# The input stage of a Mamba layer: one fp32 projection against three products of scaled fp16 parts

## The chip, the core and the metric

The kernel runs on one core of one Trainium2 chip. The core has five engines, each with its own queue of instructions: TensorE (PE: matmuls, and PEld: its weight loads), VectorE (DVE), ScalarE (ACT), GpSimd (POOL) and SyncE (SP, which here issues nearly all DMAs). They wait for one another through semaphores only. The metric is the device time of one launch in microseconds; lower is better.

## What is computed

A macaron block over x of shape (4, 2048, 256): half an attention and mixture-of-experts layer, a Mamba layer, and half an attention and mixture-of-experts layer again. The change touches only the first part of the Mamba layer, for which the reference says:

```python
h = _layernorm(_layernorm(x), norm_w, norm_b)
xz = jnp.einsum('bld,ed->bel', h, in_proj_w)        # 256 channels in, 1024 out
x, z = jnp.split(xz, 2, axis=1)                     # 512 each; x is convolved and scanned, silu(z) gates
# out = x_in + the layer's output, x_in being the first layer norm of the block's stream
```

With the norm's weight and bias written out, xz = W (w * a + b) = (W w) a + W b, where a is the normed row without weight and bias.

## The kernel before

The program is a row of phases with a barrier between them: constants, the first attention layer (three phases), `mamba_in`, two scans (forward and backward), `mamba_out`, and the second attention layer (three phases). `mamba_in` (from L1222) works on 8192 rows in 16 chunks of 512 rows. For chunk i:

- SP loads the rows (0.5 MB) into `xs`, stores `bs` (0.5 MB, stream plus normed rows, read again by `mamba_out`), `xo` (1 MB) and `zo` (1 MB). All have two buffers, by the chunk's parity.
- DVE: `statistics` (L1308) computes mean and variance and the two inverse variances; `norm` (L1327) makes the normed rows `sn` and the twice normed rows `an`; `add_base` (L1338) makes `bs`; `weigh` (L1342) reads the turned rows from PSUM, applies the norm's weight and bias, and writes `aT`; `copy_x` (L1350) moves one 128x512 tile of the x half from PSUM to `xo`, four times.
- PE: `turn` (L1380) transposes the 512x256 rows in eight 128x128 blocks; `project` (L1392) makes one 128x512 tile of the output from two fp32 matmuls (contraction 256 = 2 x 128), eight times for a chunk: x and z by turns for m = 0 to 3.
- ACT: `root` (L1412) takes the square roots of the inverse variances; `silu` (L1417) moves one tile of the z half from PSUM to `zo`, four times.
- POOL has no work in this phase.

The order is written out by hand and is the same for every chunk. PE's step i: wait for `aT` of chunk i; x0, z0, x1, z1, then `turn(i + 1)`, then x2, z2, x3, z3. DVE's step i: copy x0, norm(i + 1), copy x1, add_base(i + 1), weigh(i + 1), copy x2, statistics(i + 2), copy x3. ACT's step i: four silus, then root(i + 2). The x tiles go by turns to PSUM banks 2 and 3, the z tiles to banks 4 and 5, so a tile's matmuls wait until the tile two before it has been read. Before the first step each engine runs a prologue with the same pieces for chunk 0 and statistics(1).

The later attention phase `ffn_out` already computes its experts with three products of fp16 parts: there ACT copies the turned rows from PSUM twice (L1091 to fp32, L1094 to fp16), POOL subtracts (L983), and PE multiplies (L1045) 128x512 tiles, with other stationary operands for every matmul. `make_constants` (L81) prepares the expert weights in the same manner.

## Time and profile before

| what | value |
|---|---|
| median of 3 runs | 8745.64 us (8745.47 to 8752.05) |
| profiled execution, its own time | 8750.53 us |
| its span | 8748.8 us |
| PE, DVE, ACT, POOL busy over the span | 84%, 86%, 58%, 42% |
| the phase `mamba_in` | from about 2386 to about 2642 us of the span |

Spans of the trace are counted from the span's start. A busy PE is one whose pipeline holds a matmul; the time between the starts of two matmuls says what one of them costs. An fp32 matmul stands in the trace as two records, a transpose as one. Busy shares over the whole span mix eleven phases, so what the change is worth has to be read inside its own phase.

### The profile page before, as it was taken

What the parts mean: (1) busy time and instruction counts of PE and PEld (TensorE: products, weight loads), DVE (VectorE), ACT (ScalarE), POOL (GpSimd) and SP (SyncE); (2) the same over time, 40 slices, a digit from 0 to 9 for tenths busy, and PEclk for the clock granted to TensorE, in tenths of its full rate; (3) what the DMA queues carried; (4) which work ended last, traced back from release to release, by engine and by line L of the source; (5) the groups of instructions that cost most, each with busy time, mean ns of one, the idle gap of its engine ahead of it and who ended that gap; (6) DMA issues with size and microseconds to landing.
All of it is one profiled execution on the core that took longest, in us unless ns stands there. A gap on an engine that the chain in (4) does not pass through costs nothing. (4 is left out here: it accounts for less than half of the span.)

```text
span 8748.8 us, 137191 instructions
## 1 busy us (share of the span) xinstructions
PE 7384.9 (84%) x39098; PEld 2876.4 (33%) x39098; DVE 7557.3 (86%) x11017; ACT 5055.9 (58%) x7663; POOL 3676.0 (42%) x1812
## 2 busy tenths in 40 slices
PE   6788888889997888888878888888777888888799
PEld 3222222225543333333323333333542222222255
DVE  6898888878867999999979999999358988888888
ACT  3577777762235666666655555555224777777622
POOL 0010011100006999999969999999300100110000
PEclk8799999999999999999999999999987999999999
DMA  6001001012262222222223333333561011011122
GB/s 171 17 19 20 19 19 26 19 42 77 72 210 88 83 83 82 82 83 84 83 92 100 102 103 100 100 102 100 171 189 17 19 20 19 19 21 23 42 67 67
DMA packets 554170, 623.35 MB, mean 71 GB/s; under 512 B 205376, under 2 KB 363328, under 8 KB 549408
## 3 DMA queue, kind: packets, MB, share of 16 engines
q1 hardware_dynamic: 548896, 581.63, 22.8%
q0 software_dynamic: 4608, 33.56, 1.9%
q8 instruction: 330, 5.41, 0.3%
q14 instruction: 336, 2.75, 0.1%
HBM read 416.65 MB, written 163.76 MB: 66 GB/s over the span
## 5 line engine op out<-in xcount | busy, mean ns | idle before, releaser
L833 DVE TENSOR_REDUCE ffn_att_mx<-psum 128x1 f32<-128x512 f32 (+2 forms) x4840 | 2915.6, 655 | 389.7 <-PE psum L666 197.4
L794 ACT ACTIVATE ffn_att_e<-psum,unscale 128x1024 f32<-128x1024 f32 (+3 forms) x2560 | 2384.0, 983 | 843.9 <-PE psum L739 842.9
L632 POOL TENSOR_SCALAR_AFFINE_SELECT ffn_att_e<-ffn_att_e 128x512 f32<-128x512 f32 x512 | 324.6, 634 | 3125.8 <-ACT ffn_att_e L794 3125.8
L666 PE MATMUL psum<-ffn_att_k,ffn_att_q 48*128 48x512 f16 (+3 forms) x5384 | 989.1, 368 | 611.2 <-DVE ffn_att_mx L833 545.2
L1628 POOL TENSOR_TENSOR scan_r_h<-scan_r_h,scan_r_cs 128x1024 f32<-128x1024 f32 x512 | 1207.1, 2447 | 148.0 <-ACT scan_r_state L1791 144.7
L705 PE MATMUL psum<-ffn_att_e,ffn_att_v 128*32 128x512 f32 (+3 forms) x10240 | 1248.5, 558 | 10.0 <-issue 3.8
L1628 POOL TENSOR_TENSOR scan_f_h<-scan_f_h,scan_f_cs 128x1024 f32<-128x1024 f32 x512 | 1204.4, 2444 | 118.8 <-ACT scan_f_state L1791 116.1
L1707 PE MATMUL psum<-scan_f_h,ident 128*128 128x512 f32 x2048 | 989.0, 623 | 84.0 <-POOL scan_f_h L1628 83.1
L1707 PE MATMUL psum<-scan_r_h,ident 128*128 128x512 f32 x2048 | 975.0, 617 | 78.1 <-POOL scan_r_h L1628 77.5
L1831 ACT ACTIVATE psum<-scan_r_dt,scan_r_an 128x512 f32<-128x512 f32 x1024 | 698.1, 682 | 456.2 <-DVE scan_r_h L1923 456.0
L1831 ACT ACTIVATE psum<-scan_f_dt,scan_f_an 128x512 f32<-128x512 f32 x1024 | 697.6, 681 | 423.8 <-DVE scan_f_h L1923 423.3
L666 PEld LDWEIGHTS psum<-ffn_att_k,ffn_att_q 48*128 48x128 f16 x5384 | 263.9, 94 | 2002.3 <-DVE ffn_att_mx L833 1884.7
L1923 DVE TENSOR_TENSOR_SCAN scan_r_h<-psum,scan_r_state,scan_r_db 128x512 f32<-128x512 f32 x704 | 844.5, 1261 | 5.5 <-ACT psum L1831 5.5
L1923 DVE TENSOR_TENSOR_SCAN scan_f_h<-psum,scan_f_state,scan_f_db 128x512 f32<-128x512 f32 x704 | 840.5, 1261 | 9.0 <-ACT psum L1831 9.0
L739 PE MATMUL psum<-ffn_att_q,ffn_att_k 50*128 50x512 f16 (+3 forms) x5120 | 728.1, 355 | 32.9 <-issue 29.5
L1707 PEld LDWEIGHTS psum<-scan_f_h,ident 128*128 128x128 f32 x2048 | 384.7, 197 | 670.2 <-issue 434.1
L1707 PEld LDWEIGHTS psum<-scan_r_h,ident 128*128 128x128 f32 x2048 | 383.9, 195 | 648.8 <-issue 439.2
L1180 DVE SCALAR_TENSOR_TENSOR ffn_out_acc<-psum,ffn_out_comb,ffn_out_acc 128x256 f32<-128x256 f32 x896 | 433.4, 484 | 65.2 <-PE psum L1045 29.6
L1889 DVE TENSOR_TENSOR scan_r_db<-scan_r_du,psum 128x2048 f32<-128x2048 f32 x177 | 404.9, 2288 | 25.1 <-PE psum L1682 4.8
L1889 DVE TENSOR_TENSOR scan_f_db<-scan_f_du,psum 128x2048 f32<-128x2048 f32 x177 | 404.9, 2288 | 24.7 <-DVE scan_f_h L1923 3.9
L1923 DVE TENSOR_TENSOR_SCAN scan_f_h<-psum,scan_f_state,scan_f_dbp 128x512 f32<-128x512 f32 x320 | 385.9, 1264 | 30.8 <-ACT psum L1831 30.8
L1923 DVE TENSOR_TENSOR_SCAN scan_r_h<-psum,scan_r_state,scan_r_dbp 128x512 f32<-128x512 f32 x320 | 385.9, 1264 | 30.8 <-ACT psum L1831 30.8
(240 smaller groups left out, 9216.5 us busy)
## 6 DMA issues: line engine op xcount, KB each, us to landing
scan_f_cs<-scan_f_bcd SPq DMA_DIRECT2D x264, 256.0 KB, 3.2
scan_r_cs<-scan_r_bcd SPq DMA_DIRECT2D x264, 256.0 KB, 3.3
scan_f_bs<-scan_f_bcd SPq DMA_DIRECT2D x82, 256.0 KB, 3.5
scan_r_bs<-scan_r_bcd SPq DMA_DIRECT2D x82, 256.0 KB, 3.5
scan_f_win<-xp SPq DMA_DIRECT2D x18, 1036.0 KB, 6.6
scan_r_win<-xp SPq DMA_DIRECT2D x18, 1036.0 KB, 7.0
ffn_att_q<-q_parts SPq DMA_DIRECT2D x144, 128.0 KB, 2.9
mamba_out_ys<-yz SPq DMA_DIRECT2D x18, 1024.0 KB, 7.3
```

The lines of the kernel that those rows point to most:

```text
L632: nc.gpsimd.affine_select(out=part, in_=part, compare_op=ALU.is_ge, fill=0.0, base=0, pattern=[[0, REP], [1, P]], channel_multiplier=-1).t ...
L666: ins = nc.tensor.matmul(psum[:, turns[hh], j * w:(j + 1) * w], q[at, i // HALF, pair, i % HALF * P:(i % HALF + 1) * P], k[at, c * P:c * P ...
L705: ins = nc.tensor.matmul(psum[32 * h:32 * h + VW, BANK_O, off:CH], V[par][:, kb, :], E[:, s % PB, h, off:CH], start=kb == 0, stop=closes(s ...
L739: ins = nc.tensor.matmul(psum[:, h, off:CH], k[at, kb * P:(kb + 1) * P], q[at, qb * CH // (HALF * P), h // 2, qb * CH % (HALF * P) + off:q ...
L794: nc.scalar.activation(E[:, s % PB, 2 * hp:2 * hp + 2, off:CH], psum[:, 2 * hp:2 * hp + 2, off:CH], ACT.Exp, scale=unscale[:, 0:1]).then_i ...
L833: nc.vector.reduce_max(mx[:, hh * 2 + pairs[0]:hh * 2 + pairs[1], i // HALF, i % HALF, c // TT], psum[:, turn, 0:(pairs[1] - pairs[0]) * w ...
L1180: nc.vector.scalar_tensor_tensor(acc[:, e % 2, :], psum[:, BANKS_E[(n // 2) % 4], (e % 2) * C:(e % 2 + 1) * C], comb[par][:, t, e:e + 1], ...
L1628: nc.gpsimd.tensor_tensor(hh, hh, cs[:, n % NCS, :].unsqueeze(1).to_broadcast([P, 2, CH]), ALU.mult).then_inc(hc_ready, 1)
L1707: ins = nc.tensor.matmul(psum[:, m, :], ident[:, :], h[n % NH][:, m, :], start=False, stop=n == DS - 1)
L1831: nc.scalar.activation(psum[:, BANK_A + k % 2, :], dt[par][:, m, :], ACT.Exp, scale=an[:, m, n:n + 1]).then_inc(decay, 1)
L1889: nc.vector.tensor_tensor(db[b_turn(par, n)][:, :, :], du[par][:, :, :], psum[:, BANK_B, :].unsqueeze(1).to_broadcast([P, DM, CH]), ALU.mu ...
L1923: nc.vector.tensor_tensor_scan(h[n % NH][:, m, flip], psum[:, BANK_A + k % 2, flip], made_b[:, m, flip], state[:, n, m:m + 1], ALU.mult, A ...
```

## The change

The two operands of the projection are each written as a sum of two fp16 numbers, high and low, after scaling. The weights: W w, scaled by a factor from the largest row norm, gives `wh` and `wl`, made once, in the prologue. The rows: ACT copies the turned rows times 512 from PSUM as fp32 (`aT`) and as fp16 (`ah`), and POOL subtracts the two to give `al`. `project` makes wh·ah + wl·ah + wh·al, six fp16 matmuls for a tile where there were two fp32 matmuls. The norm's weight is now in the weights and its bias in `beta` = W b, so `weigh` is gone, and `copy_x` and `silu` apply the scale `uw` and the bias `beta` on the way out. `aT` has one buffer now, `ah` and `al` two. The factor needs sums of squares (ACT, then PE), a maximum (DVE), a root (ACT), and `beta` needs 16 small matmuls; all of that stands in the prologue.

```diff
-        aT = [sb(f"aT{p}", [P, CK, CH]) for p in range(2)]
+        aT = sb("aT", [P, CK, CH])
+        ah = [sb(f"ah{p}", [P, CK, CH], F16) for p in range(2)]
+        al = [sb(f"al{p}", [P, CK, CH], F16) for p in range(2)]
+        wh, wl = sb("wh", [P, CK, 2 * DI], F16), sb("wl", [P, CK, 2 * DI], F16)
+        sqb, onesb = sb("sqb", [P, CK, 2 * DI], BF16), sb("onesb", [P, P], BF16)
...
-                def weigh(i, par):
-                    dve.wait_ge(aT_ps, i + 1)
-                    if not (isinstance(i, int) and i < 2):
-                        dve.wait_ge(z_ps, DM * (i - 1))
+                def weights():
+                    dve.wait_ge(w_sums, 2)
+                    nc.vector.reduce_max(most[:, :], psum[:, 6:8, :].rearrange("p b n -> p (b n)"), AX.X).then_inc(w_most, 1)
+                    dve.wait_ge(w_root, 1)
+                    nc.vector.tensor_scalar(root_w[:, :], root_w[:, :], 1.0 / FULL, 1e-15, ALU.mult, ALU.add).then_inc(w_small, 1)
+                    dve.wait_ge(w_small, 2)
+                    nc.vector.reciprocal(cw[:, :], root_w[:, :]).then_inc(w_small, 1)
+                    nc.vector.tensor_scalar(uw[:, :], root_w[:, :], 1.0 / UP, None, ALU.mult).then_inc(w_small, 1)
+                    dve.wait_ge(w_small, 4)
+                    nc.vector.tensor_tensor(sc[:, :], wn[:, :], cw[:, :].to_broadcast([P, CK]), ALU.mult).then_inc(w_small, 1)
+                    dve.wait_ge(w_small, 5)
                     for k in range(CK):
-                        nc.vector.tensor_scalar(aT[par][:, k, :], psum[:, k, :], wn[:, k:k + 1], bn[:, k:k + 1],
-                                                ALU.mult, ALU.add).then_inc(aT_sb, 1)
+                        dve.wait_ge(w_high, k + 1)
+                        nc.vector.scalar_tensor_tensor(wl[:, k, :], wi[:, k, :], sc[:, k:k + 1], wh[:, k, :], ALU.mult, ALU.subtract
+                                                       ).then_inc(w_low, 1)
+                    dve.wait_ge(beta_ps, 1)
+                    nc.vector.tensor_copy(beta[:, :], psum[:, 2, 0:2 * DM]).then_inc(beta_sb, 1)
...
-                    nc.vector.tensor_copy(xo[par][:, m, :], psum[:, X_BANKS[m % 2], :]).then_inc(x_ready, 1)
+                    nc.vector.tensor_scalar(xo[par][:, m, :], psum[:, X_BANKS[m % 2], :], uw[:, 0:1], beta[:, m:m + 1],
+                                            ALU.mult, ALU.add).then_inc(x_ready, 1)
                 statistics(0, 0)
                 norm(0, 0)
                 add_base(0, 0)
-                dve.wait_ge(w_in, 48)
-                weigh(0, 0)
+                weights()
                 statistics(1, 1)
+                dve.wait_ge(beta_sb, 1)
...
                     if nxt:
                         add_base(i + 1, 1 - par)
-                        weigh(i + 1, 1 - par)
...
+            @block.gpsimd
+            def _(pool):
+                def split_low(i, par):
+                    pool.wait_ge(a_high, i + 1)
+                    if not (isinstance(i, int) and i < 2):
+                        pool.wait_ge(z_ps, DM * (i - 1))
+                    nc.gpsimd.tensor_tensor(al[par][:, :, :], aT[:, :, :], ah[par][:, :, :], ALU.subtract).then_inc(a_low, 1)
+                split_low(0, 0)
...
             @block.tensor
             def _(pe):
                 pe.wait_ge(w_in, 48)
+                pe.wait_ge(w_small, 1)
+                pe.wait_ge(w_squares, CK)
+                for b in range(2):
+                    for k in range(CK):
+                        ins = nc.tensor.matmul(psum[:, 6 + b, :], onesb[:, :], sqb[:, k, b * CH:(b + 1) * CH], start=k == 0, stop=k == CK - 1)
+                    ins.then_inc(w_sums, 1)
+                for m in range(2 * DM):
+                    for k in range(CK):
+                        ins = nc.tensor.matmul(psum[:, 2, m:m + 1], wi[:, k, m * P:(m + 1) * P], bn[:, k:k + 1], start=k == 0, stop=k == CK - 1)
+                ins.then_inc(beta_ps, 1)
...
-                        ins = nc.tensor.matmul(psum[:, bank[m % 2], :], wi[:, k, at:at + P], aT[par][:, k, :],
-                                               start=k == 0, stop=k == CK - 1)
+                        for p, (w, a) in enumerate(((wh, ah[par]), (wl, ah[par]), (wh, al[par]))):
+                            ins = nc.tensor.matmul(psum[:, bank[m % 2], :], w[:, k, at:at + P], a[:, k, :],
+                                                   start=k == 0 and p == 0, stop=k == CK - 1 and p == 2)
                     ins.then_inc(made, 1)
 
                 def step(i, par, nxt, more):
-                    pe.wait_ge(aT_sb, CK * (i + 1))
+                    pe.wait_ge(a_high, i + 1)
+                    pe.wait_ge(a_low, i + 1)
...
+                pe.wait_ge(w_low, CK)
+                pe.wait_ge(beta_sb, 1)
                 phase_steps(pe, step)
...
-                    nc.scalar.activation(zo[par][:, m, :], psum[:, Z_BANKS[m % 2], :], ACT.Silu).then_inc(z_ready, 1)
+                    nc.scalar.activation(zo[par][:, m, :], psum[:, Z_BANKS[m % 2], :], ACT.Silu, bias=beta[:, DM + m:DM + m + 1], scale=uw[:, 0:1]
+                                         ).then_inc(z_ready, 1)
+
+                def parts(i, par):
+                    act.wait_ge(aT_ps, i + 1)
+                    act.wait_ge(a_low, i)
+                    nc.scalar.activation(aT[:, :, :], psum[:, 0:CK, :], ACT.Copy, scale=UP).then_inc(aT_sb, 1)
+                    if not (isinstance(i, int) and i < 2):
+                        act.wait_ge(z_ps, DM * (i - 1))
+                    nc.scalar.activation(ah[par][:, :, :], psum[:, 0:CK, :], ACT.Copy, scale=UP).then_inc(a_high, 1)
+                act.wait_ge(w_in, 48)
+                for k in range(CK):
+                    nc.scalar.activation(sqb[:, k, :], wi[:, k, :], ACT.Square, scale=wn[:, k:k + 1]).then_inc(w_squares, 1)
                 root(0)
+                act.wait_ge(w_most, 1)
+                nc.scalar.activation(root_w[:, :], most[:, :], ACT.Sqrt).then_inc(w_root, 1)
+                act.wait_ge(w_small, 5)
+                for k in range(CK):
+                    nc.scalar.activation(wh[:, k, :], wi[:, k, :], ACT.Copy, scale=sc[:, k:k + 1]).then_inc(w_high, 1)
+                parts(0, 0)
                 root(1)
+                act.wait_ge(beta_sb, 1)
 
                 def step(i, par, nxt, more):
                     for m in range(DM):
                         silu(i, par, m)
+                        if nxt and m == 1:
+                            parts(i + 1, 1 - par)
```

Declarations of semaphores are left out; eleven are new. The orders of SP and of the stores are not changed.

## Rows read from the trace of the kernel before

**Rows 1.** Engines by stretch: length, busy us (instructions) of each, PE clock, DMA share, GB/s.

```profile
2386.00:2400.00 14.00, 2.40 (x9) 2.04 (x10) 8.40 (x28) 1.49 (x2) 0.00 (x0) 0.50 0.51 164
2400.00:2636.00 236.00, 234.92 (x632) 110.00 (x631) 155.64 (x423) 78.55 (x108) 0.00 (x0) 0.99 0.60 203
```

**Rows 2.** Waits in the phase: waiting and releasing line, us in total, times, longest.

```profile
PE psum L1397 <- DVE mamba_in_aT L1347: 1.8, 1, 1.8
```

**Rows 3.** PE in order of time, one chunk and a bit: start us, length us.

```profile
2496.41 1.04 PE L1385 MATMUL psum<-ident,mamba_in_an 128*128 128x128 f32 x8
2497.28 13.90 PE L1397 MATMUL psum<-mamba_in_aT,mamba_in_wi 128*128 128x512 f32 x32
...
2511.89 6.60 PE L1397 MATMUL psum<-mamba_in_aT,mamba_in_wi 128*128 128x512 f32 x15
```

**Rows 4.** PE in the earlier phase ffn_out: eleven fp16 matmuls, first and last.

```profile
2369.72 0.38 PE L1045 MATMUL psum<-ffn_out_eh,ffn_out_uh 128*128 128x512 f16 x1
...
2371.88 0.38 PE L1045 MATMUL psum<-ffn_out_el,ffn_out_uh 128*128 128x512 f16 x1
```

**Rows 5.** ACT and POOL splitting turned rows in ffn_out, in order of time.

```profile
2324.12 1.02 ACT L1091 ACTIVATE ffn_out_uT<-psum 128x1024 f32<-128x1024 f32 x1 [3.97 <-PE psum L1022]
2325.04 1.02 ACT L1094 ACTIVATE ffn_out_uh<-psum 128x1024 f16<-128x1024 f32 x1
...
2326.22 2.12 POOL L983 TENSOR_TENSOR ffn_out_ul<-ffn_out_uT,ffn_out_uh 128x1024 f16<-128x1024 f32 x1 [25.50 <-ACT ffn_out_uh L1094]
```

**Rows 6.** DVE in one chunk: norm, and weigh after the turn.

```profile
2487.36 0.18 DVE L1318 RECIPROCAL mamba_in_rq<-mamba_in_va 128x4 f32<-128x4 f32 x1
...
2492.07 1.38 DVE L1330 TENSOR_SCALAR mamba_in_sn<-mamba_in_xs,mamba_in_mv,mamba_in_rs 128x256 f32<-128x256 f32 x4
2493.35 1.14 DVE L1335 TENSOR_SCALAR mamba_in_an<-mamba_in_sn,mamba_in_rs 128x256 f32<-128x256 f32 x4
...
2497.48 1.53 DVE L1347 TENSOR_SCALAR mamba_in_aT<-psum,mamba_in_wn,mamba_in_bn 128x512 f32<-128x512 f32 x2 [0.77 <-PE psum L1385]
```

**Rows 7.** ACT around a root, in order of time.

```profile
2504.35 0.60 ACT L1421 ACTIVATE mamba_in_zo<-psum 128x512 f32<-128x512 f32 x1 [2.84 <-PE psum L1397]
2504.96 1.28 ACT L1415 ACT_TABLE_LOAD   x1
2506.26 0.21 ACT L1415 ACTIVATE mamba_in_rs<-mamba_in_rq 128x8 f32<-128x8 f32 x1
```

**Rows 8.** Groups of the phase: count, busy us, mean ns of one, idle before.

```profile
L1354 DVE COPY mamba_in_xo<-psum 128x512 f32<-128x512 f32 x64 | 44.0, 688 | 61.6 <-PE psum L1397 61.6
L1347 DVE TENSOR_SCALAR mamba_in_aT<-psum,mamba_in_wn,mamba_in_bn 128x512 f32<-128x512 f32 x32 | 24.5, 806 | 11.9 <-PE psum L1385 11.9
```

**Rows 9.** One stretch of 1 us inside a chunk, columns as in rows 1.

```profile
2505.00:2506.00 1.00, 1.00 (x4) 0.51 (x3) 0.00 (x0) 1.00 (x1) 0.00 (x0) 1.00 1.02 383
```

**Rows 10.** The phase's start in order of time, all engines.

```profile
2388.23 0.43 SPq L1274 DMA_DIRECT2D mamba_in_wi<-in_m_inT  x1
...
2393.89 1.38 DVE L1330 TENSOR_SCALAR mamba_in_sn<-mamba_in_xs,mamba_in_mv,mamba_in_rs 128x256 f32<-128x256 f32 x4 [0.28 <-ACT mamba_in_rs L1415]
...
2396.23 1.22 DVE L1340 TENSOR_TENSOR mamba_in_bs<-mamba_in_xs,mamba_in_sn 128x1024 f32<-128x1024 f32 x1
...
2399.54 9.38 PE L1397 MATMUL psum<-mamba_in_aT,mamba_in_wi 128*128 128x512 f32 x16 [1.78 <-DVE mamba_in_aT L1347]
```

**Rows 11.** DMA issues: KB each, median us from issue to landing.

```profile
mamba_in_wi<-in_m_inT SPq DMA_DIRECT2D x1, 1024.0 KB, 7.2
```

**Rows 12.** In the constants phase: squares, a maximum, scaled copies.

```profile
11.45 3.90 ACT L135 ACTIVATE const_sqe<-const_we,const_en 128x2048 bf16<-128x2048 f32 x2 [2.88 <-DMA const_we<-in_f_expT]
...
16.62 1.47 DVE L177 TENSOR_REDUCE const_moste<-psum 128x2 f32<-128x512 f32 x2 [7.06 <-PE psum L154]
...
20.69 6.49 ACT L141 ACTIVATE const_eh<-const_we,const_sc 128x256 f16<-128x256 f32 x16 [0.91 <-DVE const_sc L186]
```

**Rows 13.** PE in ffn_out: eight fp32 matmuls of eight columns.

```profile
2326.51 1.85 PE L1032 MATMUL psum<-ffn_out_wg,ffn_out_uT 128*128 128x8 f32 x16
```

More of the change, by code:

```diff
@@ L1232, in mamba_in @@
         bs = [sb(f"bs{p}", [P, TT, C]) for p in range(2)]
-        aT = [sb(f"aT{p}", [P, CK, CH]) for p in range(2)]
+        aT = sb("aT", [P, CK, CH])
[3 more added lines that the diff above has]
+        sqb, onesb = sb("sqb", [P, CK, 2 * DI], BF16), sb("onesb", [P, P], BF16)
+        most, root_w, cw, uw = (sb(n, [P, 1]) for n in ("most", "root_w", "cw", "uw"))
+        sc, beta = sb("sc", [P, CK]), sb("beta", [P, 2 * DM])
         xo = [sb(f"xo{p}", [P, DM, CH]) for p in range(2)]
@@ L1246, in mamba_in @@
         aT_ps, aT_sb, x_ps, z_ps = sem("aT_ps"), sem("aT_sb"), sem("x_ps"), sem("z_ps")
+        a_high, a_low = sem("a_high"), sem("a_low")
+        w_squares, w_sums, w_most, w_root, w_small, w_high, w_low, beta_ps, beta_sb = (sem(n) for n in (
+            "w_squares", "w_sums", "w_most", "w_root", "w_small", "w_high", "w_low", "beta_ps", "beta_sb"))
         x_ready, z_ready, zeroed = sem("x_ready"), sem("z_ready"), sem("zeroed")
@@ L1306, in _ @@
                 nc.vector.memset(zero[:, :, :], 0.0).then_inc(zeroed, 1)
+                nc.vector.memset(onesb[:, :], 1.0).then_inc(w_small, 1)
                 def statistics(i, par):
@@ L1374, in _, with step @@
                 phase_steps(dve, step)
+            @block.gpsimd
[6 more added lines that the diff above has]
+                split_low(0, 0)
+                def step(i, par, nxt, more):
+                    if nxt:
+                        split_low(i + 1, 1 - par)
+                phase_steps(pool, step)
             @block.tensor
@@ L1378, in _ @@
                 pe.wait_ge(w_in, 48)
+                pe.wait_ge(w_small, 1)
[8 more added lines that the diff above has]
+                ins.then_inc(beta_ps, 1)
                 def turn(i):
-                    pe.wait_ge(aT_sb, CK * i)
+                    pe.wait_ge(a_high, i)
                     for t in range(TT):
```

## Prediction

> **What bounds the kernel now.** The change lies in one phase, so I read that phase and not the shares of the whole span. First the engines by stretch [rows 1]: from 2400 to 2636 us PE is busy 234.92 of 236 us, at a granted clock of 0.99, while DVE is busy 155.64, ACT 78.55 and POOL not at all. A busy PE could still be one that is fed late, so next the waits [rows 2]: in the whole phase PE waits for the turned rows once, 1.8 us, at the start. Then PE in order of time [rows 3]: the projection starts at 2497.28 and again at 2511.89, so a chunk costs 14.61 us; the eight transposes take 0.87 (2496.41 to 2497.28), and the 32 records of the 16 fp32 matmuls the other 13.74. PE sets the pace, DVE has 155.64/236 x 14.61 = 9.6 us of work in a chunk, ACT 4.9.
>
> The start is different. The first projection record begins at 2399.54 [rows 10], with the clock at half (0.50 [rows 1]), and this first half chunk lasts 9.21 us until its transposes instead of half of 13.74, 2.3 more. As a check: 2399.54 + 16 x 14.61 - 0.87 (no turn in the last step) + 2.3 = 2634.7; the phase's PE work ends close to that, just before 2636.
>
> **The change, part by part: the loop.** PE: six fp16 matmuls per tile, 48 a chunk. Eleven such matmuls in ffn_out, each with another stationary operand, start from 2369.72 to 2371.88 [rows 4]: 2.16/10 = 0.216 us each, weight loads hidden. 48 x 0.216 = 10.37, plus 0.87 for the turn (left as it is) = 11.24 us, if nothing else is late. That saves 3.37 us a chunk, 16 x 3.37 = 53.9 us.
>
> What has to fit into 11.24 us? Let the chunk start at 0. A tile takes 1.30, so z1 is done at 5.18, the turn ends at 6.05, and the next chunk wants its `ah` and `al` at 11.24.
>
> The hand-over, the tightest. In the old kernel `weigh` starts 0.20 after the turn's end and needs 1.53 [rows 6]. Now ACT copies twice and POOL subtracts, the same operations in the same shapes as in ffn_out [rows 5]: the second copy starts 0.92 after the first, the subtraction 1.18 after that, and takes 2.12. Sum 0.20 + 0.92 + 1.18 + 2.12 = 4.42. The cover is x2, z2, x3, z3, 24 x 0.216 = 5.18. It fits with 0.76 to spare, so I cost it at nothing; without that cover it would be 4.42 a chunk. Silu z1 is queued in front of the copies on ACT, but it starts at 5.4 and ends at 6.0, before they are released. Behind them stands silu z2, due at 8.8; the copies end at 8.2.
>
> The norm of the next chunk. On ACT silu z3 of the chunk before ends at 0.8; then table load 1.28 and root 0.21 [rows 7] give 2.3. DVE's `norm` takes 2.42 (2492.07 to 2494.49 [rows 6]), so it ends near 4.8, and the turn comes at 5.18; its first block needs only the first quarter of `an`, at about 4.0. It fits, with 0.4 or more to spare.
>
> DVE: minus `weigh`, 1.53; `copy_x` grows from 0.69 to what `weigh` took for one 128x512 tile with two column operands, 0.81 [rows 8], so + 0.5 a chunk. 9.6 - 1.5 + 0.5 = 8.6 of 11.24. ACT: + 1.02 + 1.02, and four silus with scale and bias, which no row shows: 0.60 as now [rows 7] or 0.69, the old copy's; I take 0.65. 4.9 + 2.0 + 0.2 = 7.1 of 11.24. POOL 2.1. The x and z banks: every tile's reader ends at least 1 us before the bank is wanted. All hidden behind PE.
>
> Does a Copy between two silus make ACT load a table? No row has this pair. In ffn_out the copies follow other functions with no load in front of them [rows 5]; nothing is my value. The other end is a load of 1.28 [rows 7] before the copies: the hand-over becomes 5.70, 0.52 late, 8 us over 15 chunks.
>
> DMA: no transfer is added or moved. A chunk still moves 3.15 MB. Now that is 203 GB/s [rows 1]; in 11.24 us it is 280. Inside a chunk the queues reach 383 GB/s at a full share [rows 9] and then stand still, so 3.15/0.383 = 8.2 us of transfer fit. Stores have a whole chunk to land, loads more. Hidden.
>
> **The change: the prologue.** Here nothing hides. Old: weights issued at 2388.23, landing 7.2 later [rows 10, 11], 2395.4; `norm` from 2393.89; projection at 2399.54. New, along the longest chain:
> - ACT waits for the weights, then squares 2 x 1024 columns. 2048 columns took 1.95 [rows 12]; half that and a fixed part, 1.1 each: 2397.6. root(0) is queued behind them, and needs its table after Square: 1.28 + 0.21, 2399.1. So `norm` starts at 2399.15, 5.3 late.
> - From `norm`'s start to the end of `add_base` took 3.56 (2393.89 to 2397.45 [rows 10]): 2402.7.
> - The maximum over 1024 columns stands behind `add_base` on DVE: two of 512 took 1.47 [rows 12], I take 1.3: 2404.0. PE's sums were ready long before.
> - Root 0.25, then four dependent small operations of 0.2 (0.18 and the gap [rows 6]): 2405.1.
> - `wh`: 256 columns took 0.41 [rows 12]; 1024 I take at 1.1, the mean of a plain 1.02 [rows 5] and a bit more; twice: 2407.3.
> - parts(0) and the subtraction, 0.92 + 1.18 + 2.12 = 4.2: 2411.5. With half a microsecond for semaphores the projection starts at 2412.0.
>
> Beside it: `beta`'s 16 matmuls, 32 records. Sixteen of eight columns took 1.85 [rows 13] at full clock, so 3.7, or 7.4 at half; with four matmuls of sums in front and the first turn behind they end between 2404 and 2408.5. `wl` runs on DVE until 2408.7 (1.22 for a tile of this size [rows 10]), `beta`'s copy and statistics(1) after it until 2411.8. None is later than 2412, but PE at half clock comes within a microsecond of the copies.
>
> Cost 2412.0 - 2399.54 = 12.5. Bounds: 10 if the clock has risen for the first chunk too (it would give back 2.3), 16 if PE's own chain at half clock decides and ACT's pieces come out at their upper ends. What the half clock costs in the first chunk I take as the same 2.3, since PE stands still before it in both kernels.
>
> The end of the phase is as before (last stores, then the barrier); eleven more semaphores to clear, 0 to 0.5, taken at 0. Nothing behind the phase reads other data.
>
> **Table loads: row and rule.** The profile shows no time between a silu's end (2504.95), the table load and the root at 2506.26 beyond the load's 1.28 [rows 7]. The Trainium skill (ScalarE: Activation LUTs, What ACT_TABLE_LOAD costs) counts a drain of 1.38 us with each switch; by that the prologue would be an estimated 1.4 us longer. The trace does not agree with it here, so it gets no chance of its own.
>
> **Rivals.** A, the forecast: PE alone sets the pace, 11.24 a chunk.
>
> B, the hand-over or the norm is late. What speaks for it: only 0.76 and some 0.4 us of room, and POOL enters a loop in which DVE reads SBUF. If the subtraction has to stand behind a DVE operation of two SBUF tensors, the longest is `add_base`, 1.22 [rows 10]: 1.22 - 0.76 = 0.46 late, 15 x 0.46 = 7 us. Against: `add_base` should be over at 6.9 and the subtraction start at 8.4. With the table load 8. With both, (1.22 + 1.28 - 0.76) x 15 = 26. So B gives 8711 to 8730, centre 8713. The Trainium skill has a rule for this (SBUF — State Buffer, Who interferes with whom): a GpSimd instruction and a DVE one with two SBUF inputs exclude each other for their whole length. It names a mechanism for B; in the order above they don't meet.
>
> C, DMA becomes the limit. The mean before is 203 GB/s; if it couldn't go over, say, 226, a chunk would take 13.9, the loop would win 11 and the prologue lose 12.5: 8747, no change. Against it stands 383 in the bursts [rows 9].
>
> D, the other side: fp16 products are not at 0.216 here, because every one has its own weight load and would have to end before the next begins. It decides from (14.61 - 0.87 - 12.5/16)/48 = 0.27 us each. With the record's own length, 0.38 [rows 4], as the interval: 48 x 0.38 + 0.87 = 19.1 a chunk, 8745.6 + 16 x 4.5 + 12.5 = 8830. Against: the same rows show such a sequence, with changing weights, at 0.216.
>
> **How the numbers follow.** Saving 53.9 - 12.5 = 41.4. The profiled execution took 8750.5, 4.9 more than the median of the runs; its like would be 8709.1, and on the median 8745.6 - 41.4 = 8704. The likeliest case's own range is 8698 to 8711: the prologue's bounds give - 2.5 and + 3.5, rounding of the matmul interval and the runs' own scatter the rest. Chances: A 0.70; B 0.19, of it 0.16 below 8728; C and anything else that eats the gain 0.06; D or another loss 0.05. The range that leaves out no more than 2 in 10 reaches from 8698 into B, to 8722. A measurement of this kernel tells some 0.2% (17 us) from no change, so faster is below 8728: A and most of B, 0.86; within 0.2%: 0.09; slower: 0.05.
>
> **What would show it.** In the new trace: projection starts 11.2 apart, matmuls 0.216 apart; PE without waits in the loop; the first projection near 2412, its last near 2593; POOL's subtraction ending 4.4 after the turn; no table load between silu and copy. Wrong would make it: PE waiting for POOL or ACT in every chunk; a prologue over 16; a granted clock under 1 in the loop; matmuls further apart.

## The result and the profile after

| | before | after |
|---|---|---|
| median of 4 runs each, beside one another | 8745.56 us (8740.5 to 8752.05) | 8700.63 us (8693.87 to 8704.81) |
| ratio to before | | 0.9945, 95% interval 0.993 to 0.9959 |
| profiled execution, own time and span | 8750.53, 8748.8 us | 8693.87, 8692.0 us |
| `mamba_in`, first load to first load of the scan | 255.7 us | 215.8 us |
| the same chunk, turn to turn | 14.61 us | 11.23 us |
| projection starts after the phase's first load | 12.8 us | 26.2 us |
| second attention, first load of `ffn_in` to load of `ffn_out`'s weights | 1900.8 us | 1882.2 us |

The changed kernel is faster by 45 us in this comparison, and by 65 and 49 us in two later ones. The predicted saving was 41.4 us. The engines by stretch, columns as in [rows 1], over the prologue and the body of the phase in the changed kernel:

```profile
2386.00:2412.00 26.00, 9.91 (x43) 9.00 (x44) 12.61 (x41) 8.01 (x9) 0.62 (x1) 0.50 0.47 123
2412.00:2590.00 178.00, 176.26 (x865) 87.07 (x866) 140.90 (x384) 116.84 (x135) 33.42 (x16) 0.98 0.76 261
```

PE is still what fills the body, 176.26 of 178 us; DVE has 140.90 and ACT 116.84. DMA moves 261 GB/s at a share of 0.76, against 203 before [rows 1], and nothing waits for it there. PE in order of time, the rows that answer to [rows 3]:

```profile
2488.70 1.04 PE L1429 MATMUL psum<-ident,mamba_in_an 128*128 128x128 f32 x8
2489.57 0.38 PE L1442 MATMUL psum<-mamba_in_ah,mamba_in_wh 128*128 128x512 f16 x1
...
2494.76 0.38 PE L1442 MATMUL psum<-mamba_in_ah,mamba_in_wh 128*128 128x512 f16 x1
...
2499.93 1.04 PE L1429 MATMUL psum<-ident,mamba_in_an 128*128 128x128 f32 x8
```

Two turns are 11.23 us apart, two matmuls 0.216 ((2494.76 - 2489.57)/24). The 24 matmuls after the turn end, and the next chunk starts, at 2494.76. The waits of the phase say the same: all that PE waits for in front of its projection is one wait, at the start.

```profile
PE psum L1442 <- POOL mamba_in_al L1402: 4.4, 1, 4.4
```

The other engines in the same chunk, in order of time:

```profile
2488.91 0.78 ACT L1469 ACTIVATE mamba_in_zo<-psum,mamba_in_beta,mamba_in_uw 128x512 f32<-128x512 f32 x1 [0.79 <-PE psum L1442]
2489.85 1.02 ACT L1475 ACTIVATE mamba_in_aT<-psum 128x1024 f32<-128x1024 f32 x1 [0.17 <-PE psum L1429]
2490.77 1.02 ACT L1478 ACTIVATE mamba_in_ah<-psum 128x1024 f16<-128x1024 f32 x1
...
2491.95 2.13 POOL L1402 TENSOR_TENSOR mamba_in_al<-mamba_in_aT,mamba_in_ah 128x1024 f16<-128x1024 f32 x1 [9.18 <-ACT mamba_in_ah L1478]
...
2493.76 0.35 DVE L1326 TENSOR_SCALAR mamba_in_va<-mamba_in_mv 128x4 f32<-128x4 f32 x1
```

The turn ends at 2489.57, the low part at 2494.08: 4.51 us after it, and 0.68 before the next chunk's start. Of the 0.68 some 0.24 is spent between POOL's end and PE's start, as the prologue's rows below show (2413.50 to 2413.74). No table load stands between the silu and the copies. The last row is a statistic of four columns a row that takes 0.35 us and ends 0.03 us after POOL does; more on it below. The groups, columns as in [rows 8]:

```profile
L1374 DVE TENSOR_SCALAR mamba_in_xo<-psum,mamba_in_uw,mamba_in_beta 128x512 f32<-128x512 f32 x64 | 51.6, 806 | 32.7 <-PE psum L1442 32.7
L1469 ACT ACTIVATE mamba_in_zo<-psum,mamba_in_beta,mamba_in_uw 128x512 f32<-128x512 f32 x64 | 49.8, 778 | 59.4 <-PE psum L1442 59.2
...
L1326 DVE TENSOR_SCALAR mamba_in_va<-mamba_in_mv 128x4 f32<-128x4 f32 x16 | 6.3, 396 | 0.6
```

The prologue, all engines in order of time, answers to [rows 10]; the phase's first load is at 2387.55 here, the weights are issued at 2389.00:

```profile
2396.71 2.19 ACT L1481 ACTIVATE mamba_in_sqb<-mamba_in_wi,mamba_in_wn 128x1024 bf16<-128x1024 f32 x2 [37.46 <-DMA mamba_in_wi<-in_m_inT]
2398.91 1.28 ACT L1463 ACT_TABLE_LOAD   x1
...
2400.45 1.38 DVE L1340 TENSOR_SCALAR mamba_in_sn<-mamba_in_xs,mamba_in_mv,mamba_in_rs 128x256 f32<-128x256 f32 x4 [6.10 <-ACT mamba_in_rs L1463]
2400.70 6.83 PE L1421 MATMUL psum<-mamba_in_bn,mamba_in_wi 128*128 128x1 f32 x32
...
2403.93 1.22 DVE L1354 TENSOR_REDUCE mamba_in_most<-psum 128x1 f32<-128x1024 f32 x1
...
2406.05 2.19 ACT L1487 ACTIVATE mamba_in_wh<-mamba_in_wi,mamba_in_sc 128x1024 f16<-128x1024 f32 x2 [0.67 <-DVE mamba_in_sc L1361]
...
2407.39 1.95 PE L1429 MATMUL psum<-ident,mamba_in_an 128*128 128x128 f32 x8
2409.37 1.02 ACT L1475 ACTIVATE mamba_in_aT<-psum 128x1024 f32<-128x1024 f32 x1 [1.13 <-PE psum L1429]
...
2411.38 2.12 POOL L1402 TENSOR_TENSOR mamba_in_al<-mamba_in_aT,mamba_in_ah 128x1024 f16<-128x1024 f32 x1 [54.72 <-ACT mamba_in_ah L1478]
2411.74 1.79 DVE L1326 TENSOR_SCALAR mamba_in_va<-mamba_in_mv 128x4 f32<-128x4 f32 x1
...
2413.74 0.60 PE L1442 MATMUL psum<-mamba_in_ah,mamba_in_wh 128*128 128x512 f16 x1 [4.41 <-POOL mamba_in_al L1402]
```

ACT was ready for its copies at 2408.24, when `wh` was done, but the turned rows came only at 2409.34: for the last 1.13 us PE at half clock (granted 0.50) sets the time.

Of the 56.8 us between the two profiled spans, the phase accounts for 39.9. The second attention, whose code is the same in both, is 18.6 us shorter, and all the rest 1.7 longer. The experiments are for both: is the phase's 39.9 what the prediction says it is, and what are the 18.6?

### The profile page after: what moved, and what is told of

The parts are those of the page before. It is cut to its first block and busy times, and to the rows that moved or that the text cites. A ratio compares the mean times of both kernels' runs of the same rounds, so it can differ in the third digit from the quotient of the medians.

```text
span 8692.0 us, 137865 instructions
## 1 busy us (share of the span) xinstructions
PE 7318.7 (84%) x39389; PEld 2857.4 (33%) x39390; DVE 7547.6 (87%) x10994; ACT 5104.9 (59%) x7700; POOL 3709.9 (43%) x1828
```

## The experiments

"Phase" is the length of `mamba_in` as in the table, "second attention" that stretch of the table, and "first attention" the same stretch of the first attention layer, which runs ahead of `mamba_in` and of every edit. All three come from one profiled execution of each kernel, and the time is the median of its runs. In the two profiles of the table above the first attention took 1885.6 us before and 1886.2 after.

| kernel | time | ratio to before [95%] | phase | first attention | second attention |
|---|---|---|---|---|---|
| same_again | 8690.68 | 0.9928 [0.9914, 0.9941] | 216.1 | 1880.3 | 1882.4 |
| same_third | 8691.52 | 0.9943 [0.9929, 0.9956] | 213.5 | 1888.0 | 1881.0 |
| split_twice | 8725.34 | one run | 241.7 | 1892.8 | 1882.4 |
| folded_fp32 | 8747.54 | 0.999 [0.9981, 1.0] | 265.4 | 1890.6 | 1881.1 |
| root_first | 8687.67 | 0.992 [0.9906, 0.9933] | 210.0 | 1896.1 | 1882.8 |
| root_first_third | 8693.02 | 0.9941 [0.9928, 0.9955] | 209.6 | 1885.4 | 1879.6 |
| two_products | 8674.74 | one run | 189.5 | 1891.3 | 1882.9 |
| dve_split | 8697.56 | one run | 213.2 | 1884.2 | 1889.7 |
| root_first_dve_split | 8697.44 | 0.9951 [0.9939, 0.9963] | 209.1 | 1884.4 | 1890.6 |
| changed_32_more | 8704.84 | one run | 216.8 | 1892.9 | 1885.4 |
| before_again | 8753.99 | one run | 256.2 | 1891.0 | 1897.7 |
| before_third | 8765.25 | one run | 255.6 | 1893.6 | 1902.6 |
| before_8_more | 8759.92 | one run | 255.7 | 1893.7 | 1901.6 |
| before_36_more | 8745.88 | 0.9994 [0.9985, 1.0004] | 259.9 | 1890.7 | 1878.8 |
| before_dve_4us | 8749.09 | 1.0002 [0.9993, 1.0011] | 259.3 | 1888.4 | 1884.1 |
| before_dve_4us_again | 8734.75 | one run | 259.5 | 1882.1 | 1882.8 |

The median of the kernel before beside them was 8755.86 us for same_again, split_twice, folded_fp32 and root_first; 8750.49 for before_again, before_36_more, two_products and dve_split; 8744.91 for root_first_dve_split, before_dve_4us, before_8_more and changed_32_more; 8740.83 for the rest.

### Is the hand-over hidden, and by how much?

**split_twice** lets POOL subtract twice, so that the low part is 2.1 us later:

```diff
+                    nc.gpsimd.tensor_tensor(al[par][:, :, :], aT[:, :, :], ah[par][:, :, :], ALU.subtract).then_inc(a_once, 1)
+                    pool.wait_ge(a_once, i + 1)
                     nc.gpsimd.tensor_tensor(al[par][:, :, :], aT[:, :, :], ah[par][:, :, :], ALU.subtract).then_inc(a_low, 1)
```

> GpSimd does its subtraction twice in every chunk, the second after the first; nothing else differs. Theory 1 (the hand-over is hidden with 0.67 us of room): one more 2.17 us makes it 1.5 late in every chunk, so a chunk takes 12.7 instead of 11.23, and the phase 215.8 + 2.2 (prologue) + 15 x 1.5 = 240.5 us. Rival (there is far more room, or TensorE isn't waiting for this): the phase is 218.

The phase took 241.7 us, 25.6 more than the changed kernel beside it, and the chunk below 12.97 instead of 11.23 (the others of the loop 12.8 to 13.0). POOL and PE in order of time in this kernel:

```profile
2496.21 2.13 POOL L1402 TENSOR_TENSOR mamba_in_al<-mamba_in_aT,mamba_in_ah 128x1024 f16<-128x1024 f32 x1 [8.45 <-ACT mamba_in_ah L1480]
2498.42 2.12 POOL L1404 TENSOR_TENSOR mamba_in_al<-mamba_in_aT,mamba_in_ah 128x1024 f16<-128x1024 f32 x1
```

```profile
2493.04 1.04 PE L1431 MATMUL psum<-ident,mamba_in_an 128*128 128x128 f32 x8
...
2500.83 0.39 PE L1444 MATMUL psum<-mamba_in_ah,mamba_in_wh 128*128 128x512 f16 x1 [1.57 <-POOL mamba_in_al L1404]
...
2506.01 1.04 PE L1431 MATMUL psum<-ident,mamba_in_an 128*128 128x128 f32 x8
```

The second subtraction starts 2.21 after the first, and the chunk (2493.04 to 2506.01) is 1.74 longer than 11.23. So the changed kernel has 0.47 us of room here and 0.59 in the chunks of 12.85, and its own rows say much the same (0.68 less 0.24). Had the hand-over been the limit, the whole 2.21 would have come through.

### What do the fp16 products alone give, and what the folding costs?

**folded_fp32** has the new prologue, with the weight and bias folded and scaled as in the changed kernel, but one fp32 product; there is no split.

```diff
-                        for p, (w, a) in enumerate(((wh, ah[par]), (wl, ah[par]), (wh, al[par]))):
-                            ins = nc.tensor.matmul(psum[:, bank[m % 2], :], w[:, k, at:at + P], a[:, k, :],
-                                                   start=k == 0 and p == 0, stop=k == CK - 1 and p == 2)
+                        ins = nc.tensor.matmul(psum[:, bank[m % 2], :], ws[:, k, at:at + P], aT[par][:, k, :],
+                                               start=k == 0, stop=k == CK - 1)
```

> The fold alone: norm weight and scale in the weights, bias beta, scale and bias applied by copy_x and silu, but fp32 weights and fp32 rows in two fp32 matmuls per tile, one ScalarE copy of the turned rows, no GpSimd. Theory 1 (the gain is TensorE's, from fewer passes): a chunk takes 14.61 us as before, the prologue is some 10 us longer than before (13.4 in the changed kernel, less the second copy and the subtraction), so the phase is 266 us, 10 longer than before. Rival (part of the gain comes from taking weigh off VectorE): the phase is under 255.

The phase took 265.4 us, 9.7 more than before, and a chunk is back at 14.61:

```profile
2498.39 1.04 PE L1409 MATMUL psum<-ident,mamba_in_an 128*128 128x128 f32 x8
...
2513.00 1.04 PE L1409 MATMUL psum<-ident,mamba_in_an 128*128 128x128 f32 x8
```

So the loop's whole gain is in the products, and the folding only costs. But the total did not go up with the phase: it lies 8.3 us under before's. Another 18 us have come from elsewhere, in a kernel without a single fp16 product in this phase, as far as the median of the kernel before beside it, 8755.86 us and the highest of all, can be trusted; more on it below.

**two_products** leaves wl·ah out, so its output lacks that part; it asks what binds once PE has a third less to do.

```diff
-                        for p, (w, a) in enumerate(((wh, ah[par]), (wl, ah[par]), (wh, al[par]))):
+                        for p, (w, a) in enumerate(((wh, ah[par]), (wh, al[par]))):
...
-                                                   start=k == 0 and p == 0, stop=k == CK - 1 and p == 2)
+                                                   start=k == 0 and p == 0, stop=k == CK - 1 and p == 1)
```

> The changed kernel without the product of low weights and high rows (left out of the computation), 32 matmuls a chunk in place of 48. TensorE's own work is 32 x 0.216 + 0.87 = 7.8 us a chunk, but the cover of the hand-over shrinks to 16 x 0.216 = 3.5, under its 4.5. Theory 1: the hand-over (and right beside it the chain silu, table, root, norm, turn, 8.7) now sets the pace, 3.5 + 0.9 + 4.6 = 8.9 to 9.3 a chunk; the phase is 181 to 186. Rival (TensorE is still the limit and the hand-over isn't close): 7.8 a chunk and 161.

A chunk took 9.71 us in the mean and the phase 189.5, more than the expectation. Engines over the body, then waits over the phase:

```profile
2412.00:2560.00 148.00, 124.05 (x588) 58.09 (x588) 137.18 (x383) 111.22 (x132) 31.89 (x15) 0.96 0.89 290
```

```profile
ACT L1463 <- DVE mamba_in_rq L1335: 14.0, 14, 1.3
PEld psum L1429 <- DVE mamba_in_an L1345: 11.8, 13, 1.1
PE psum L1442 <- POOL mamba_in_al L1402: 10.7, 7, 4.4
PE psum L1442 <- issue: 8.6, 9, 1.0
DVE mamba_in_sn L1340 <- ACT mamba_in_rs L1463: 9.0, 15, 6.2
```

DVE is now busy 137.18 of 148 us. PE waits for it before the turn, and some 1.0 us in front of each projection for the low part too (in the lines of POOL and of "issue" by turns). But from 2431 to 2560 us DVE waits for PE nowhere: it stands still 0.2 us a chunk for the root (2.8 of the 9.0; the other 6.2 are the prologue's) and otherwise only between its own operations. So DVE's own sequence, with the table load and root beside it, sets the pace. The prediction's 8.6 us of DVE work a chunk is busy time; with these waits, and the 0.2 us that a statistic loses to POOL, the sequence takes 9.7. The changed kernel is thus 1.5 us a chunk away from its next limit, and that limit is DVE's.

### The split on DVE, and the order of the prologue

**dve_split** drops ACT's fp32 copy and POOL's subtraction; DVE makes the low part straight from PSUM.

```diff
+                    nc.vector.scalar_tensor_tensor(al[par][:, :, :], psum[:, 0:CK, :], UP, ah[par][:, :, :], ALU.mult, ALU.subtract
+                                                   ).then_inc(a_low, 1)
...
-                    nc.gpsimd.tensor_tensor(al[par][:, :, :], aT[:, :, :], ah[par][:, :, :], ALU.subtract).then_inc(a_low, 1)
...
-                    nc.scalar.activation(aT[:, :, :], psum[:, 0:CK, :], ACT.Copy, scale=UP).then_inc(aT_sb, 1)
```

> The subtraction of the changed kernel on VectorE, from PSUM (1.28 us in the row of ffn_in with this shape), in place of GpSimd's 2.13; ScalarE's fp32 copy goes. The hand-over falls from 4.5 to about 2.6, VectorE's work rises from 8.9 to 10.2 of 11.23. Theory 1 (TensorE sets the pace, the hand-over is free): a chunk stays 11.23, only the prologue is shorter by 1.8; the phase is 214. Rival (GpSimd and VectorE get in each other's way in the loop and cost time, or VectorE is too full): below 210, or above 216.

213.2 us for the phase, 11.23 a chunk: a shorter hand-over buys nothing in the loop. In the prologue it takes 11.44 us from `norm` to the first projection, where all three profiles of the changed kernel take 13.29: 1.85 us less. The length of the phase alone would not show that: the third profile of the changed kernel has 213.5 us as well, with a `norm` that came 1.2 us earlier and a first chunk less slowed by the clock. The group of the statistic in dve_split shows what POOL did to it in the changed kernel:

```profile
L1325 DVE TENSOR_SCALAR mamba_in_va<-mamba_in_mv 128x4 f32<-128x4 f32 x16 | 2.7, 170 | 0.5
```

**root_first** keeps every operation and changes the order of the prologue: ACT takes root(0) before the squares, PE turns chunk 0 before the sums and `beta`, ACT splits chunk 0 before it makes `wh`.

```diff
+                turn(0)
                 pe.wait_ge(w_in, 48)
                 pe.wait_ge(w_small, 1)
...
-                turn(0)
...
+                root(0)
                 act.wait_ge(w_in, 48)
...
-                root(0)
+                parts(0, 0)
                 act.wait_ge(w_most, 1)
...
-                parts(0, 0)
                 root(1)
```

> The changed kernel with the prologue in another order: ScalarE takes the root of chunk 0 before it waits for the weights and squares them, and splits the rows of chunk 0 while the sums run; TensorE turns chunk 0 before the sums and beta. Theory 1 (the prologue's 13.4 us is a chain on the path): the projection starts about 20.7 us after the phase's first load instead of 26.2, right behind beta's matmuls, and the phase is 210.3, the total 5.5 us under the changed kernel. Rival (the order costs a table load for Square, or the weights' chain is as long anyway): projection at 25 or later, no gain.

The phase took 210.0 us, as expected, 6.1 less than the changed kernel beside it. In its prologue the first load is at 2400.34, `norm` at 2407.44, 7.1 after it where the changed kernel needs 12.9:

```profile
2407.44 1.38 DVE L1340 TENSOR_SCALAR mamba_in_sn<-mamba_in_xs,mamba_in_mv,mamba_in_rs 128x256 f32<-128x256 f32 x4 [0.28 <-ACT mamba_in_rs L1462]
...
2413.63 6.82 PE L1432 MATMUL psum<-mamba_in_bn,mamba_in_wi 128*128 128x1 f32 x32
2421.24 0.61 PE L1441 MATMUL psum<-mamba_in_ah,mamba_in_wh 128*128 128x512 f16 x1 [0.79 <-DVE mamba_in_beta L1368]
```

What ends last is now `beta`'s 6.82 us of PE at half clock. In the total the 6 us can't be told: against the changed kernel in the same comparison it was 3.0 us faster, and the second time 1.5 slower.

> The changed kernel with the reordered prologue, again. mamba_in 210.0; on the same chip the total 6 us under same_third by the phase alone. Theory L: second attention 1882. Theory E: any value from 1880 to 1901.

The phase took 209.6 us, and that is only 3.9 less than the changed kernel's 213.5 beside it, for the reason given above. In the start of the projection, counted from the first load, the two pairs say 5.5 and 4.6 us. The total shows neither.

**root_first_dve_split** joins both edits.

> Both improvements together: the prologue in the order of root_first, the subtraction on VectorE from PSUM as in dve_split. Theory 1: in root_first the projection starts when beta's matmuls end, 20.9 us after the phase's first load, so the shorter split of chunk 0 gives nothing more; a chunk stays 11.23; the phase is 210.0 (within 0.5), 45.7 under the kernel before. The whole kernel should be the fastest so far, 8685 to 8695. Rival (the split of chunk 0 was on the path too): 208 or less.

The phase took 209.1 us, the shortest with all three products, again behind `beta`; the expectation had 210.0 within 0.5, and the 0.9 less stands within what the start of a phase moves by itself. Its total, 8697.44 us, missed the expected 8685 to 8695: 47.5 us under before's, it is what the phase gives (46.6) and no more.

### Where do the other 18 us come from?

First, is the difference in the second attention repeatable? The kernel before and the changed one were run and profiled again, unchanged.

> The changed kernel once more, unaltered. Phase length means from the first row load of mamba_in to the first window load of the forward scan: 255.76 us before, 215.82 after. Theory 1: only this phase is changed, so the phase is again 215.8 (within 0.5) and the total is 40 us below the kernel before, ratio 0.9954; what the first measurement showed beyond that (48 by the ratio 0.9945) is scatter of the attention phases. Theory 2: the change also shortens something behind the phase, and the ratio is again 0.9945 or less.

> The kernel before once more, unaltered, for its profile. Both attention phases do the same work. In the profile before, the second took 1900.8 us (first load of ffn_in to the output weights of ffn_out) with the clock at half for long, in all five profiles of changed kernels 1881 to 1883; the first took 1880 to 1896 in all. Theory S (scatter): the second attention of this kernel comes out anywhere between 1880 and 1900. Theory P (the program before and the changed ones differ there in a lasting way): 1900 again, within 2.

> The changed kernel unaltered, a third time. Theory L (the surplus in the second attention is lasting): the total is 55 to 60 us under the kernel before (40 from mamba_in, 15 to 20 from the second attention) and the profile shows 1882 there. Theory E (it comes and goes between executions and chips): the difference lies nearer 40, or the profile shows another value.

> The kernel before, its third profile. Theory L: second attention 1898 to 1901. Theory E: may be under 1890 this time.

In these profiles it is. The kernel before takes 1900.8, 1897.7 and 1902.6 us for it, the changed one 1882.2, 1882.4 and 1881.0. By the totals the changed kernel lies 65 and 49 us under the kernel before in the repeats, where theory 2 of same_again had 48 or more and theory L 55 to 60. The chip does not make the difference: 1897.7 was taken on the same chip as 1878.8 (before_36_more, below), and 1902.6 on the same as 1881.0. But the first attention, which nothing has touched, moves too: 1880.3 to 1896.1 us over the eighteen profiles, 1880.3, 1886.2 and 1888.0 in the changed kernel alone, and 1896.1 and 1885.4 in root_first and its repeat. Engines over a stretch of 1900 us there, first of the kernel before:

```profile
6379.20:8279.20 1900.00, 1549.91 (x13397) 491.05 (x13397) 1626.83 (x2995) 1285.08 (x1475) 163.32 (x258) 0.93 0.16 35
```

and of the changed one:

```profile
6340.70:8240.70 1900.00, 1539.63 (x13421) 492.81 (x13421) 1628.86 (x3003) 1290.09 (x1487) 164.56 (x260) 0.94 0.17 38
```

The code there is the same. PE does 24 more instructions in 10 us less, at a mean granted clock of 0.94 for 0.93. Summed over the clock's records, the kernel before spends 262, 253 and 268 us of it at the 1.2 GHz level, the changed one and the others under 1886 spend 210 to 221, and the two at 1890 spend 238 and 239, and before_8_more (below, 1901.6) 256. So what differs is how long PE is at its lower level. The first attention shows the same tie inside one program: 195 us at the lower level where it took 1880.3 and 224 where it took 1886.2 (changed kernel), 223 and 254 where it took 1885.4 and 1896.1 (root_first). No run shows which of the two, clock or length, follows the other.

Does it need the change at all? **before_36_more** is the old kernel with `beta`'s 16 matmuls (32 records; the 36 of its name is a slip) put behind the first turn, as an unused product.

```diff
                 turn(0)
+                for m in range(2 * DM):
+                    for k in range(CK):
+                        nc.tensor.matmul(psum[:, 6, m:m + 1], wi[:, k, m * P:(m + 1) * P], bn[:, k:k + 1], start=k == 0, stop=k == CK - 1)
```

> The kernel before with 32 more matmul records in mamba_in's prologue on TensorE (a product of the weights and the bias into a PSUM bank that nobody reads), so that every later TensorE instruction has another place in the program; no fp16, nothing else moved. The phase mamba_in should be 255.8 plus at most 6.8. Theory P1 (the place in the program sets how long the clock is at half in the second attention): the second attention takes 1882 as in the changed kernels, and the total is some 12 us below the kernel before although mamba_in is longer. Rival P2 (what counts is the changed phase itself, its length or its work): 1900, and the total is 3 to 7 us above.

It does not: 1878.8 us there, in one profile, with the old products. The total, expected some 12 us below the kernel before, was 4.6 below. **before_dve_4us** adds some 4 us to the old phase on DVE alone, with not one more instruction on PE, and **before_8_more** adds 8 records on PE (the loop of before_36_more with `range(2)` for `range(2 * DM)`) without making the phase longer. **changed_32_more** has the same 32 records put into the changed kernel, behind its first turn.

```diff
+                for p in range(2):
+                    nc.vector.memset(xo[p][:, :, :], 0.0).then_inc(padded, 1)
+                dve.wait_ge(padded, 2)
                 dve.wait_ge(w_in, 48)
                 weigh(0, 0)
```

> The kernel before with some 4 us more of VectorE work in mamba_in's prologue (two memsets of xo) and not one TensorE instruction more: mamba_in becomes about 4 us longer, as in before_36_more, but every TensorE instruction keeps its place in the program. Theory P1 (the place of TensorE's instructions decides about the 18 us in the second attention): the second attention takes 1898 to 1901, and the total is some 4 us above the kernel before. Rival P3 (any shift in time or in any engine's code removes them): 1879 to 1883, total 14 us below.

> The kernel before with only 8 more matmul records in the prologue in place of 32. Theory P1 in its wide form (any move of TensorE's instructions does it): second attention near 1880. Narrow form (it depends on how far they move): anywhere from 1880 to 1901. mamba_in 255.8 plus at most 2.

> The kernel before with two more memsets on VectorE, again. Theory L: 1884 again, within 3. Theory E: may be 1895 to 1902 this time, which would say that the same program goes both ways.

> The changed kernel with 32 more matmul records in its prologue. mamba_in becomes 216 plus about 2 to 3 us. Theory P1, narrow form (some places are good and some bad): the second attention may be anywhere from 1880 to 1901. Wide form (the place of the kernel before is the only bad one): 1882 again.

Engines over 1900 us of the second attention, first of before_dve_4us, then of before_8_more:

```profile
6387.90:8287.90 1900.00, 1539.08 (x13421) 492.71 (x13421) 1627.54 (x3000) 1287.43 (x1482) 164.55 (x260) 0.94 0.16 37
```

```profile
6386.80:8286.80 1900.00, 1544.31 (x13397) 490.45 (x13397) 1626.21 (x2994) 1285.09 (x1475) 163.31 (x258) 0.93 0.16 35
```

The first goes with the changed kernel (1884.1 and 1882.8 us), the second with the one before (1901.6). changed_32_more stays with its own kind, 1885.4, with a phase of 216.8 us. So adding PE instructions ahead of the stretch is not needed for the shorter length, and 8 records do not bring it: theory P1 in its wide form falls. In both old kernels whose phase is some 4 us longer the stretch is short; in the one whose phase kept its 255.7 us it stayed long. That is in line with a shift in time that decides, but no run separates such a shift from other effects of an edit, and why some microseconds, 3,700 us earlier, should settle how long the clock stays down is open.

The totals confirm this in part only. By the medians, before_dve_4us is 4.2 us slower than before with a phase 3.6 longer, before_36_more 4.6 faster with a phase 4.2 longer, folded_fp32 8.3 faster with one 9.7 longer: a rest of -1, 9 and 18 us, where the profiles show 17 to 22 less in the second attention. For before_dve_4us the total came out as P1 had it, and only the profile as P3. The changed kernel's rest is 45, 65 and 49 less the phase's 40: 5, 25 and 9.

And the record speaks against a lasting property of the program. Besides its three profiles the kernel before has 58 runs, from 8730.92 to 8767.04 us: one program, 36 us apart. Its third profile took 8765.25 us, 16 more than the slowest of the nine runs beside it (8736.52 to 8749.2), so it does not stand for them. Give every phase the shortest length that any of the seven profiles of the kernel before and its variants shows, and the second attention 1897.7 us, its shortest in a profile of the kernel before: the sum is an estimated 8741.9 us. 16 of the 58 runs took less. In those runs the second attention was shorter than in any of the three profiles, or another phase shorter than in any of the seven. So three profiles at 1898 to 1903 us do not show that the kernel before is always there, and how much of the 18.6 us belongs to the edit and how much to the execution is open. So is why PE stays longer at the lower level in one execution than in another.

## Why the prediction was right, and where it was off

**The loop.** Right to 0.01 us: 11.23 a chunk against 11.24, matmuls 0.216 apart, PE without a wait. Predicted 53.9 for 16 chunks; 16 x 3.38 = 54.1. folded_fp32, back at 14.61, shows that the products alone make it.

**The hand-over and the norm.** Right: hidden. The room was 0.44 to 0.59 where 0.76 was predicted; the prediction left out the time from POOL's end to PE's start, 0.24. split_twice measured the room from the other side. No table load comes between silu and copy. B, C and D did not happen; DMA rose to 261 GB/s with nobody waiting.

**Sizes beside the path.** `copy_x` 0.81 as predicted. Silu with scale and bias took 0.78, over my bounds of 0.60 and 0.69: 0.13 x 4 a chunk on ACT, hidden. DVE's statistic waits for POOL in every chunk (0.27 to 0.35 for 0.17), hidden too. That DVE's sequence needs 9.7 my sum of busy time (8.6) did not show.

**The prologue.** 13.4 us against 12.5, in bounds. The chain up to `wh` came within 0.2 us of the sum, counted from the phase's first load. The missing piece is the one that the prediction named and left at nothing: PE at half clock, which was 1.13 us late with the first turn; from the first copy to the projection it then took 4.37 where 4.7 was taken, which gives 0.3 back. The first chunk at half clock cost 2.4 us (from 2413.74 to 2494.76 are 7 chunks of 11.23 and 2.4), 2.3 were taken. root_first and its repeat show that about 5 of the 13.4 were order and not work (5.5 and 4.6).

**The end of the phase.** Taken at 0, it was 0.6: from the end of PE's last matmul to the scan's first load 7.6 us before and 8.2 after. So 54.1 - 13.4 - 0.6 = 40.1 accounts for the phase as a whole: 39.9 saved, 41.4 predicted.

**The step that failed** is the last one of the sum: "Nothing behind the phase reads other data", taken to mean that every other phase keeps its time, and with it the term of the range for that, 3.5 us downwards for "rounding of the matmul interval and the runs' own scatter" (8704 - 2.5 - 3.5 = 8698). The predicted 8704 lies 3 us above the measured 8700.63. By the ratio, which is taken against before's runs beside it, the changed kernel comes out at 0.9945 x 8745.56 = 8697.5 (8684 to 8710 by its interval), just under the range; the two repeats give 8682.6 and 8695.7 on the same footing, lower still. The mechanism of the phase was right. That the total came so near is partly luck: the phase gave 1.5 us less than predicted, and the rest of the program 5 more than nothing.

What the runs showed in its place: the other phases read the same data and run the same code, and still the total fell by 45, 65 and 49 us where the phase gives 40. The second attention was 18.6 us shorter in the profile, between 1878.8 and 1902.6 in all; the first attention, ahead of the change, moved by 16 us; the median of the kernel before alone lay between 8740.83 and 8755.86 us in the five comparisons. In the profiles the lengths of both attention stretches go with the time at the lower clock, and the shorter second one doesn't need the fp16 products. By the medians a term of some 15 us (an estimate) for the rest of the program was due instead of 3.5. What triggers it is not settled.

## What to carry to other kernels

Where PE is gapless over fp32 matmuls, three 16-bit products in their place are worth 0.859 - 3 x 0.216 = 0.21 us for each 128x128x512 product (0.859: 13.74/16), as long as the split is issued under matmuls that don't need it; 4.5 us of split and 0.24 to start PE want at least 22 of the 16-bit matmuls (0.216 each) behind the turn. Order a new prologue by its longest chain before counting its work: root, turn and split of chunk 0 ahead of the weights' chain were together worth 5 of 13 us. And before a few tenths of a per cent are put down to a change, read an untouched phase in both profiles, and in more than one profile of each kernel: a difference there need not be the change's own, and it can be half as large as the effect.

## What the hardware showed that was not expected

- **A small DVE operation held by POOL.** A tensor_scalar of 128x4 takes 0.17 us alone and 1.79 while POOL subtracts in the prologue (2411.74 to 2413.53, POOL's end 2413.50), 396 ns in the mean of the phase against 170 in dve_split, where POOL is idle. The Trainium skill (SBUF — State Buffer, Who interferes with whom) says that a tensor_scalar can enter a mode with two ports and then shuts GpSimd out, or is shut out by it, for the whole instruction. The runs agree, and that the operation is tiny does not spare it; no run shows which mode it ran in. The statistics and their aggregate, next to it in the same stretch, keep their 0.41 and 0.16 us.
- **Activations with a column as scale.** 128x512 with scale and bias columns 0.78 us, without 0.60 [rows 7]; 128x1024 with a scale column 1.10 for a Square or Copy in SBUF (2.19 for two), 1.02 for a plain Copy from PSUM.
- **The clock of an untouched phase.** The same code, the second attention, took 1898 to 1903 us in four profiles and 1879 to 1891 in fourteen, with a mean granted clock of 0.93 in the first and 0.94 in those of the others that are shown. The four programs that were profiled more than once stayed on their side there, but the first attention moved by up to 11 us inside one program, and 16 of 58 runs of the kernel before are too short for the second attention of its profiles.
